# A cross-attention block: five moves within the written order of a software-pipelined loop

## The reference

```python
x = layer_norm(hidden, ln1_w, ln1_b)
q, k, v = x @ q_w + q_b, ctx @ k_w + k_b, ctx @ v_w + v_b     # 16 heads of 32
attn = softmax(where(mask, q @ k.T / sqrt(32), lowest))
hidden = (attn @ v) @ cproj_w + cproj_b + hidden
y = gelu(layer_norm(hidden, ln2_w, ln2_b) @ fc_w + fc_b)      # 512 -> 2048
out = hidden + y @ proj_w + proj_b                            # 2048 -> 512
```

## Time and profile before

| | |
|---|---|
| median of 3 runs | 764.95 us (764.66 to 768.26) |
| the profiled execution's own time | 765.3 us |
| its span, first to last instruction | 763.5 us |
| attention part | to about 400 us |
| mean granted TensorE clock | 0.963 |
| TensorE busy | 703.7 us |
| VectorE, ScalarE, GpSimd busy | 460.8, 322.2, 251.0 us |

### The profile page before, as it was taken

One profiled execution on the slowest core, in us unless ns is written; L12 is line 12 of the kernel. 1 busy time (PEld: TensorE's weight loads), 2 busy tenths in 40 slices (PEclk: granted clock), 3 DMA queues, 4 the chain that ended last, 5 costly groups with the idle time before them and its releaser, 6 DMA issues.

```text
span 763.5 us, 13145 instructions
## 1 busy us (share of the span) xinstructions
PE 703.7 (92%) x4544; PEld 610.1 (80%) x4544; DVE 460.8 (60%) x860; ACT 322.2 (42%) x581; POOL 251.0 (33%) x217
## 2 busy tenths in 40 slices
PE   4489989899998989999889999999999999999998
PEld 3378879798888889888667888888888888888886
DVE  5367978988788897978877766442325223151213
ACT  4237766867676686757652121112211121211110
POOL 3505656655545665655752212000000001000000
PEclk9788989999999999999889999999999999999999
DMA  9756554644455464434604500010001000010001
GB/s 247 203 139 176 160 159 123 166 138 154 139 153 153 124 168 111 135 103 143 180 30 125 165 1 1 0 56 1 2 0 56 0 0 0 0 55 1 1 0 57
DMA packets 51130, 69.16 MB, mean 91 GB/s; under 512 B 8328, under 2 KB 29192, under 8 KB 51088
## 3 DMA queue, kind: packets, MB, share of 16 engines
q1 hardware_dynamic: 50816, 68.07, 30.8%
q0 software_dynamic: 272, 0.54, 0.4%
HBM read 47.21 MB, written 20.99 MB: 89 GB/s over the span
## 4 chain that ended last, share of the span: by engine, by line
PE 68%; issue 10%; POOL 6%; DVE 5%; DMA 4%; SPq 3%; ACT 3%; DVEq 0%; ACTq 0%; POOLq 0%
PE psum L1172 8%; PE psum L1174 8%; PE psum L1173 8%; PE psum L1159 7%; PE psum L1157 7%; PE psum L1158 7%; PE psum L975 5%; PE psum L977 5%; PE psum L976 5%; POOL p_lo L462 5%; PE psum L1009 2%; DMA stacks<-qk_rows 2%; PE psum L1059 2%; DMA qk_rows<-qk 2%; PE psum L993 1%
## 5 line engine op out<-in xcount | busy, mean ns | idle before, releaser
L462 POOL TENSOR_TENSOR p_lo<-p,p_hi 128x512 f16<-128x512 f32 x128 | 156.0, 1228 | 137.6 <-ACT p_hi L535 137.3
L662 ACT ACTIVATE h<-psum,cols 128x512 f32<-128x512 f32 x64 | 44.1, 690 | 290.0 <-PE psum L1159 290.0
L913 DVE CAST h_hi<-h 128x512 fp32r<-128x512 f32 x64 | 27.6, 432 | 207.3 <-ACT h L662 207.3
L533 ACT ACTIVATE p<-psum,maskbias 128x512 f32<-128x512 f32 x128 | 88.3, 690 | 47.2 <-PE psum L993 46.1
L1172 PE MATMUL psum<-w_mlp,h_hi 128*128 128x512 f32 x256 | 100.7, 393 | 0.9 <-DVE hidden L758 0.9
L1174 PE MATMUL psum<-w_mlp,h_lo 128*128 128x512 f32 x256 | 99.7, 390 | 0.0
L1173 PE MATMUL psum<-w_mlp,h_hi 128*128 128x512 f32 x256 | 99.7, 390 | 0.0
L1157 PE MATMUL psum<-y_hi,w_mlp 128*128 128x512 f32 x256 | 99.7, 389 | 0.0
L1159 PE MATMUL psum<-y_hi,w_mlp 128*128 128x512 f32 x256 | 99.7, 389 | 0.0
L1158 PE MATMUL psum<-y_lo,w_mlp 128*128 128x512 f32 x256 | 99.6, 389 | 0.0
L535 ACT ACTIVATE p_hi<-psum,maskbias 128x512 f16<-128x512 f32 x128 | 88.8, 694 | 0.0
(11 more groups left out here) (104 smaller groups left out, 1514.2 us busy)
## 6 DMA issues: line engine op xcount, KB each, us to landing
qk_rows<-qk SPq DMA_DIRECT2D x32, 512.0 KB, 2.7
stacks<-qk_rows SPq DMA_DIRECT2D x64, 256.0 KB
stacks<-qk_rows SPq DMA_DIRECT2D x64, 128.0 KB
hidden<-in_x_dram SPq DMA_DIRECT2D x8, 512.0 KB, 4.4
ctx_sb<-in_ctx_dram SPq DMA_DIRECT2D x8, 512.0 KB, 5.3
w_mlp_raw<-in_L_xattn_fc_w_dram SPq DMA_DIRECT2D x16, 256.0 KB, 4.5
w_mlp_raw<-in_L_xattn_proj_w_dram SPq DMA_DIRECT2D x16, 256.0 KB, 6.2
out_dram<-hidden SPq DMA_DIRECT2D x16, 256.0 KB, 2.1
```

The costliest lines, as they stand in the source:

```text
L462: pool.tensor_tensor(p_lo[:, slot, :], p32[:, u % 2, :], p_hi[:, slot, :], ALU.subtract).then_inc(s["p_lo_done"], 1)
L533: act.activation(p32[:, u % 2, :], psum[:, ST + kc, :], ACT.Exp, bias=maskbias[:, kc:kc + 1], scale=SCALE32)
```

## The change

Five places move, and none of the arithmetic does. ScalarE: in step 0 the first exponentials come behind both ctx copies. TensorE: in step 0 the order ctx 0, values, ctx 1, scores becomes ctx 0, scores, ctx 1, values; in step 2 the scores stand in the middle of the v projection, after the first six of its twelve matmuls (two of the four k), and not ahead of it. VectorE: the third part of v is made for kc = 0 in step 0, where both were, and for kc = 1 in step 1 behind `low_parts`; in step 3 the residual add stands between the reductions of heads 0 and 1, and v32 - v1 comes before `affine_x` and the reductions of heads 2 and 3, not after them. `v_split` counts two a batch.

```diff
--- before.py
+++ after.py
@@ -614,9 +614,9 @@
                 if g == 0:
                     if batch(it + 1):
                         context_hi(it, 0)
-                    exps(it, g, 0)
                     if batch(it + 1):
                         context_hi(it, 1)
+                    exps(it, g, 0)
                     exps(it, g, 1)
                     maxima_out(it, g)
                     if batch(it + 1) and not (isinstance(it, int) and it == -1):
@@ -671,7 +671,7 @@
                     for t in (2 * g - 4, 2 * g - 3):
                         affine(0, t, t)
                 if it == B and g == 1:
-                    wait(act, "v_split", B)
+                    wait(act, "v_split", B * 2)
                     gelu(0, 0)
 
             iterations(act, step, weights=weights, tail=tail)
@@ -760,7 +760,7 @@
             def add_values(it, t):
                 b = it + 1
                 wait(dve, "v_proj", b * 2 + (t + 1))
-                wait(dve, "v_split", b)
+                wait(dve, "v_split", b * 2)
                 dve.tensor_tensor(v32[:, t, :], in_bank("v", t), vb_bc[:, :], ALU.add).then_inc(s["v_added"], 1)
 
             def low_parts(it, g):
@@ -814,8 +814,15 @@
                                       axis=AX.X, op=ALU.add).then_inc(s["pv_taken"], 1)
                     dve.reciprocal(rl[:, t, h0:h0 + GH], rows[:, :, 0]).then_inc(s["pv_taken"], 1)
 
+            def third_part(kc):
+
+                dve.tensor_tensor(vparts[:, kc, :, 1 + 2 * HD:VW], v_heads[:, kc],
+                                  vparts[:, kc, :, 1 + HD:1 + 2 * HD], ALU.subtract).then_inc(s["v_split"], 1)
+
             def step(it, g):
                 low_parts(it, g)
+                if g == 1 and batch(it):
+                    third_part(1)
                 if isinstance(it, int) and (it, g) == (-1, 1):
                     mask_columns()
                 if isinstance(it, int) and (it, g) == (-1, 0):
@@ -836,15 +843,15 @@
                     ln2_norm(3, 3)
                 if g != 1:
                     products_out(it, g)
-                maximum(it, g, (0, 1))
+                maximum(it, g, (0,))
+                if g == 3 and batch(it - 1):
+                    add_hidden(it, 0)
+                maximum(it, g, (1,))
                 if g == 0 and batch(it + 1) and not (isinstance(it, int) and it == -1):
                     x_lo(it + 1)
                 if g == 0 and batch(it):
                     wait(dve, "v_cast", it * 2 + 1)
-                    for kc in range(KC):
-                        ins = dve.tensor_tensor(vparts[:, kc, :, 1 + 2 * HD:VW], v_heads[:, kc],
-                                                vparts[:, kc, :, 1 + HD:1 + 2 * HD], ALU.subtract)
-                    ins.then_inc(s["v_split"], 1)
+                    third_part(0)
                 if g == 1 and batch(it - 1):
                     b = it - 1
                     for j in range(2):
@@ -869,15 +876,13 @@
                 if isinstance(it, int) and (it, g) == (B - 1, 3):
                     weights(1)
                     split_y(0)
-                if g == 3 and batch(it - 1):
-                    add_hidden(it, 0)
+                if g == 3 and batch(it + 1):
+                    wait(dve, "v1_cast", it + 2)
+                    dve.tensor_tensor(v32[:, :, :], v32[:, :, :], v1[:, :, :], ALU.subtract).then_inc(s["v_rest"], 1)
                 if g == 3 and batch(it + 2):
                     affine_x(it + 2)
                 if not last:
                     maximum(it, g, (2, 3))
-                if g == 3 and batch(it + 1):
-                    wait(dve, "v1_cast", it + 2)
-                    dve.tensor_tensor(v32[:, :, :], v32[:, :, :], v1[:, :, :], ALU.subtract).then_inc(s["v_rest"], 1)
 
             def weights(i):
 
@@ -968,10 +973,12 @@
 
         @block.tensor
         def _(pe):
-            def three_passes(out_ap, pairs):
+            def three_passes(out_ap, pairs, between=None):
 
                 n = len(pairs)
                 for i, (a_hi, a_lo, b_hi, b_lo) in enumerate(pairs):
+                    if between and i == n // 2:
+                        between()
                     nc.tensor.matmul(out_ap, a_hi, b_hi, start=(i == 0), stop=False)
                     nc.tensor.matmul(out_ap, a_hi, b_lo, start=False, stop=False)
                     ins = nc.tensor.matmul(out_ap, a_lo, b_hi, start=False, stop=(i == n - 1))
@@ -1030,13 +1037,16 @@
                                          src[:, 0, k, :], src[:, 1, k, :]) for k in range(KT)])
                 ins.then_inc(s["qk_proj"], 1)
 
-            def project_v(it, t):
+            def project_v(it, t, between=None):
                 if not batch(it + 1):
+                    if between:
+                        between()
                     return
                 wait(pe, "w_lo_v", 1)
                 bank = bank_of(it, "v", t)
                 three_passes(bank, [(cs[:, 0, k, t * P:(t + 1) * P], cs[:, 1, k, t * P:(t + 1) * P],
-                                     w_att[:, 2, 0, k, :], w_att[:, 2, 1, k, :]) for k in range(KT)]).then_inc(s["v_proj"], 1)
+                                     w_att[:, 2, 0, k, :], w_att[:, 2, 1, k, :]) for k in range(KT)],
+                             between).then_inc(s["v_proj"], 1)
 
             def project_c(it, t):
                 b = it - 1 - t
@@ -1067,7 +1077,7 @@
                     return
                 b = it - 1 if g == 0 else it
                 wait(pe, "p_lo_done", (G + 1) * 4)
-                wait(pe, "v_split", b + 1)
+                wait(pe, "v_split", (b + 1) * 2)
                 wait(pe, "v_cast", (b + 1) * 2)
                 gp = (g - 1) % NG
                 for t in range(TT):
@@ -1104,9 +1114,9 @@
                 transposed_scores(it, g, 0)
                 if g == 0:
                     transposes(it, "ctx", 0, it + 1, ctx_sb, "ctx_loaded", 16, "ctx_tr")
+                    scores(it, g, (0, 1))
+                    transposes(it, "ctx", 1, it + 1, ctx_sb, "ctx_loaded", 16, "ctx_tr")
                     values(it, g)
-                    transposes(it, "ctx", 1, it + 1, ctx_sb, "ctx_loaded", 16, "ctx_tr")
-                    scores(it, g, (0, 1))
                     transpose_max(it, g)
                     if last:
                         transposed_scores(it, g, 1)
@@ -1124,8 +1134,7 @@
                 if g == 2:
                     transpose_max(it, g)
                     values(it, g)
-                    scores(it, g, (0, 1))
-                    project_v(it, 1)
+                    project_v(it, 1, lambda: scores(it, g, (0, 1)))
                 if g == 3:
                     transpose_max(it, g)
                     values(it, g)
```

## The result

The changed kernel took 771.83 us in the median of 20 runs (768.03 to 777.85), the kernel before 766.40 us in 20 runs beside them (763.32 to 772.68). The ratio is **1.0077 (95% interval 1.0057 to 1.0097)**: the change makes the kernel 0.8% slower, some 6 us; the forecast was 0.5%. The profiled execution of the changed kernel took 769.1 us, its span is 767.3 us, 3.8 us more than before. The ratios leave out runs that are more than 1.5% above the fastest of the same kernel: there are none but five of the 17 of the kernel before in the last experiment.

The account below looks back on a forecast made before the run. TensorE, busy 92%, was taken as the bound, with time to win only where it idles or runs at its lower clock. Terms 2.8 + 1.4 + 0.25 + 0.3 - 0.1 - 1.1 + 0.6 = +4.1 us gave 769.0 us, range 766 to 772.5.

Parts of the forecast that it names:

- Step 0's order: ctx copies together on ScalarE move x_hi 1.14 us later; TensorE's 0.81 us gap becomes 0.6 + 0.3 us, gain 0.
- The first iteration: Iteration 0: scores waiting for their fill now head the chain, loss 2.8 us; step (0,1) values wait, loss 1.4 us.
- Iteration 1: No gap covers its waits: x_lo loses 0.25 us, at most 1.2, and the moved L845 piece 0.3 us.
- x_lo against GpSimd: Step 0, L792 meets GpSimd's att product: TensorE waits 0.15 us if VectorE is first, 1.15 us if GpSimd is.
- The third part: Step 1: L738 stays blocked by GpSimd, maxima gap gains 0.1 us; -0.1 us in total over iterations 2 to 6.
- rival 1: TensorE's gap before step 1's transposed maxima closes, L738 done before 237.5: 755 us, faster; chance 0.10.
- The fills: SP's queue behind the column maxima, including the next stack's fills, runs 1.1 us later in unchanged order; no price given.
- Step 3: Residual add moves 0.6 us forward, closing TensorE's gap ahead of the x transposes: 1.1 us gained together.
- Step 2: Scores within the v projection: the projection needs its bank at once, may wait 0.1 us; 0.6 us lost over all.
- Rival 2: The gap stays or splits, but the stretches at 1.2 GHz go: 762 us; chance 0.17.
- rival 4: Steady iterations lose too: GpSimd wins the port at x_lo, or three more 1.7 us stretches: 774 us, slower; chance 0.15.

Follow-up runs that it names:

- the last experiment: Changed kernel with ScalarE's step-0 order as before and the residual of steps (6,3) and (7,3) behind the second maximum as before: 756.94 us, ratio 0.9957.

## Why the prediction was right, and where it was wrong

The forecast, slower by 0.5%, has the right sign and is 0.3% short; 771.83 lies in the range. The first two iterations, which carry the sum, went as forecast in kind. That the rest came out near is luck: the terms leave about -0.6 us for it, the profiles show -0.8, but made of other things, a gain on the clock and losses that were priced at nothing. The largest gain in the change, the 0.9% of the third part, was priced at 0.1 us. The steps fared as follows.

**Step 0's order, right, and the cause.** The copies together on ScalarE put x_hi 1.13 us later behind the second copy (1.14 forecast), and the end of GpSimd's work of the step 0.8 us later. One run shows that ScalarE's order alone loses 0.8%, a second that undoing it turns 1.0077 into 0.9942, a third that undoing TensorE's half gains nothing.

**The first iteration, right.** The projection 6.65 us behind the scores' release: a loss of 2.81 against 2.8. The values 1.0 against 1.4. By the table's marks, which stand behind these scores, the first step loses 1.9 us, the second 1.5 (it takes 10.5 us and more in every kernel with the third part in two pieces, 9.0 to 10.1 in the four without) and the other two 1.1.

**Iteration 1, too small.** 0.25 + 0.3 was forecast, 1.3 measured. TensorE waited 2.20 us for the projection, 0.74 before, and 0.67 us for its stack, where it had not waited. The step that failed is the choice between the forecast's two ends of x_lo, "0.25 us, at most 1.2". Here GpSimd's product came first, by 0.01 us, and L792 took 2.13 us (VectorE, then GpSimd, step (1,0)):

```profile
103.24 2.13 DVE L792 TENSOR_TENSOR xs<-x_t,xs 128x1024 fp32r<-128x1024 f32 x1 [0.52 <-ACT xs L586]
```

```profile
103.23 1.05 POOL L455 TENSOR_TENSOR att<-att,rl 128x512 f32<-128x512 f32 x1
```

The forecast had 1.15 us for that end, and with its 0.3 that is 1.45, near the 1.3.

**x_lo against GpSimd, right in five iterations.** VectorE came first in iterations 0 and 2 to 5, and L792 took 1.23 us. In iterations 1 and 6 GpSimd did, and it took 2.13. It is so in all five kernels with ScalarE's new order.

**The third part, right in this kernel, and for the reason given.** L738 had to sit out a GpSimd instruction in the changed kernel (1.07 us), as forecast; but one and not two. The prediction's "it has to sit out both" misread, where two instructions stand in one row: the second of them began at 248.97, 0.07 us ahead of L738, as here 0.10:

```profile
248.97 1.17 POOL L462 TENSOR_TENSOR p_lo<-p,p_hi 128x512 f16<-128x512 f32 x1
```

The Trainium skill says in "SBUF — State Buffer", section "SBUF: two separate sides", that the port pair of VectorE and GpSimd is locked for a whole instruction; the trace agrees, with 1.07 us and an end 0.02 us behind that of the one instruction. The gap was to shrink by 0.1 us, though, and shrank by 0.6. L738 was done 9.95 us behind the start of the second ctx copy, against 10.34 before: that is 0.4 of it; the rest is TensorE's own and I did not trace it. What I had not drawn from my own later start of GpSimd is that this blocking is ScalarE's doing. I took rival 1, the gap closes, for a question about the third part; with ScalarE's old order it does close, to 0.3 us, and the four iterations are 7.8 us shorter than before (8.6 with the third part alone).

**The fills, not priced.** The prediction says that SP's queue is 1.1 us later and attaches no price. There is a new wait of 0.6 to 0.7 us ahead of the scores of step 1 in iterations 2 to 4, and in step (7,1) one of 2.10 us (0.32 before). That the later queue makes it is not shown: in step (4,1) ScalarE's order alone has none, and the seven kernels with ScalarE as before and the third part in two pieces have 0.15 to 0.66 us of it.

**Step 3, wrong in sign.** -1.1 us was forecast. The gap went, as forecast; with the maxima's gap beside it that gave 0.2 us over iterations 2 to 5. What failed is the sentence that the last iteration costs 0, for want of ctx transposes: there the residual's wait holds the MLP's splits back, 2 to 3 us where the last stretch shows it.

**Step 2, right in kind, its size open.** 0.6 us was forecast, and the ratios show none. In the profiles step 2 takes 9.6 to 9.7 us from its maxima to those of step 3 in iterations 0 to 5 of every kernel with this edit, and 9.0 in every one without; the rest of the iteration gives a part back. Iterations 2 to 5 take 169.4 us with it and the third part, and 167.9 with the third part alone.

**Rival 2, in part.** The stretches at half clock in iterations 3 to 6 went from four to one. Iterations 3 to 6 of the changed kernel, with the granted clock behind the five engines (columns as in the windows above); before it is 0.96 in each of the four:

```profile
189.00:233.92 44.92, 42.16 (x374) 38.06 (x371) 36.49 (x71) 30.43 (x56) 25.53 (x21) 0.96 0.51 142
233.92:277.42 43.50, 40.61 (x374) 36.50 (x371) 36.37 (x71) 30.32 (x56) 25.52 (x21) 1.00 0.52 147
277.42:320.01 42.59, 40.28 (x374) 36.46 (x370) 36.27 (x71) 30.32 (x56) 25.51 (x21) 1.00 0.49 138
320.01:362.30 42.29, 38.98 (x357) 34.98 (x354) 33.77 (x64) 29.99 (x55) 26.74 (x22) 1.00 0.44 122
```

By the forecast's own price of 1.7 us each that gave back 5.1 us, 3.4 of it before (6,0). The kernel with the order of before in iteration 0 has the same instructions in iterations 2 to 5, three stretches there instead of one, and takes 177.5 us against 174.6: so the price is nearer 1.5, and how many stretches there are differs from one execution to the next. Iterations 2 to 5 are only 1.9 us shorter, and (6,0) to (7,2) not at all, so some 2.5 to 3 us were lost beside them, 1.8 of it perhaps in step (7,1), whose wait for the stack grew by that much; where the rest went stays open. So rival 4, the steady iterations lose too, was in part at work at the same time: GpSimd won the port at x_lo in iteration 6, but there were not more stretches at 1.2 GHz. The sentence that the prediction takes from "TensorE: Matmul & The Clock Gate" of the Trainium skill, Part 1, is about when a lowered clock comes back, and not about how often it falls; the count of stretches neither bears it out nor speaks against it. One sign of being wrong did show, an iteration under 43 us, if only from (5,0) to (6,0), 42.6 us.

## What to carry to other kernels

An operation that is moved on one engine is to be followed to every engine that starts on its output, and each is to be compared with what it will now run beside. Here 1.1 us on ScalarE made GpSimd end behind VectorE's last small instruction, and iterations 2 to 5 take 174.6 us with it and 168.7 without, 1.5 us an iteration, a part of which is the one stretch at half clock. A set of edits that sum to a small loss can hold one worth 0.9%: run them alone. And in a software-pipelined loop an order that is right in the middle is to be looked at again in the first and the last iteration, where the operation that it waits for comes at another time.

## What the runs showed of the hardware

A small VectorE instruction of 128x8 elements took 0.17 us with GpSimd done and 1.07 us when it started 0.10 us behind the start of a 128x512 operation of GpSimd's of 1.15 us, in the same place of the same loop; which of the two it was hung on 1.1 us on a third engine.

The granted clock in the four iterations from (2,0) to (6,0) of each kernel, by TensorE's largest single gap: with one of 1.7 us in each iteration there were three or four stretches at 1.2 GHz (before 3, step 0's order alone 3, ScalarE's order alone 4, step 3 alone 4); with one of 1.1 us in each, one to three (changed 1, TensorE as before 2, iteration 0 as before 3); with none above 0.93 us (the seven kernels with ScalarE as before and the third part in pieces) none. TensorE's idle time sorts the kernels with stretches from those without as well: it is 10.8 to 12.9 us in the seven kernels that have stretches and 6.3 to 8.6 in the seven that have none, so these runs don't tell which of the two matters. A gap of 1.1 us is no sure price either way: the same loop got one stretch or three.
